# The last graph-attention layer: five weight-side fills instead of nine, the residual product in each unit, and a new order of the side work

## The reference, cut to what matters

```python
h = jnp.maximum(_layernorm(x), 0.0)
Wh = h @ W                                   # 64 x 64
src = Wh @ a[:64]; dst = Wh @ a[64:]
e = leaky_relu(src[:, :, None] + dst[:, None, :], 0.2)
e = where(adj > 0, e, NEG_INF)
attention = softmax(e, axis=-1)              # 1024 x 1024 per graph
h_prime = einsum('bij,bjf->bif', attention, Wh) + h @ W_res
h_prime = elu(h_prime)
x = x + (h_prime - mean) * rsqrt(var + eps) * gamma + beta
```

## Time and profile before

| what | us |
|---|---|
| median of 3 runs (3599.07 to 3604.4) | 3600.49 |
| the profiled execution's own time | 3603.63 |
| its span | 3601.8 |
| start of the last layer on DVE | 3229.28 |
| first transpose of unit 0 of graph 0 | 3260.52 |
| end of the last unit's product | 3584.23 |

### The profile page before, as it was taken

One profiled execution on the slowest core, in us unless ns is written; L12 is line 12 of the kernel. 1 busy time (PEld: TensorE's weight loads), 2 busy tenths in 40 slices (PEclk: granted clock), 3 DMA queues, 4 the chain that ended last, 5 costly groups with the idle time before them and its releaser, 6 DMA issues. The chain is left out here.

```text
span 3601.8 us, 78158 instructions
## 1 busy us (share of the span) xinstructions
PE 3093.4 (86%) x31127; PEld 1693.5 (47%) x31127; DVE 3058.1 (85%) x4734; ACT 2921.4 (81%) x3521; POOL 1005.8 (28%) x565
## 2 busy tenths in 40 slices
PE   7987998999999969888898898988988988878785
PEld 5664666666666633333333333333333333336664
DVE  6666777777787779999999999999999999965765
ACT  4665777777777759999999999999999999966665
POOL 4433665556655600000000100000000000005654
PEclk9998999999999979999999999999999999988988
DMA  7630000000000000000000000000000000002111
GB/s 244 214 129 20 21 21 21 19 21 20 18 19 23 16 10 10 10 10 10 10 10 10 10 10 10 10 10 10 10 10 10 10 10 10 10 17 59 53 53 36
DMA packets 68315, 111.44 MB, mean 31 GB/s; under 512 B 26372, under 2 KB 26502, under 8 KB 67974
## 3 DMA queue, kind: packets, MB, share of 16 engines
q1 hardware_dynamic: 67974, 106.67, 9.7%
HBM read 86.59 MB, written 18.87 MB: 29 GB/s over the span
## 5 line engine op out<-in xcount | busy, mean ns | idle before, releaser
L1029 ACT ACTIVATE l_scalar_ring<-l_w,l_r 128x1024 f32<-128x1024 f32 x1632 | 1716.8, 1161 | 40.4 <-DVE l_values L1075 29.5
L1143 DVE TENSOR_SCALAR l_vector_ring<-l_w_code,l_r_code 128x2048 f32<-128x2048 f32 x1232 | 1590.0, 1359 | 3.5 <-issue 0.6
L966 PE MATMUL scores<-l_scalar_ring,l_signs 128*32 128x512 f32 x6528 | 791.1, 603 | 93.8 <-ACT l_scalar_ring L1029 93.5
L976 PE MATMUL scores<-l_vector_ring,l_signs_code 128*32 128x512 f16 x9856 | 675.4, 396 | 133.8 <-DVE l_vector_ring L1143 132.9
L242 ACT COPY probs_t<-turned 128x512 f32<-128x512 f32 x576 | 325.6, 589 | 435.0 <-PE turned L201 434.8
L450 POOL TENSOR_TENSOR l_masked<-l_relu,mask 128x1024 f32<-128x1024 f32 x256 | 546.1, 2134 | 421.8 <-ACT l_relu L607 390.4
L976 PEld LDWEIGHTS scores<-l_vector_ring,l_signs_code 128*32 128x32 bf16 x9856 | 243.3, 96 | 586.9 <-DVE l_vector_ring L1143 296.3
L212 PE MATMUL outT<-probs_t,l_values 128*64 128x128 f32 x6144 | 430.5, 283 | 88.0 <-ACT probs_t L242 47.4
L212 PEld LDWEIGHTS outT<-probs_t,l_values 128*64 128x64 f32 x6144 | 341.5, 139 | 239.4 <-DVE l_acc L695 95.4
L269 ACT ACTIVATE l_probs<-l_logits,negmax 128x1024 f32<-128x1024 f32 x384 | 443.8, 1156 | 7.6 <-DVE negmax L260 7.6
L201 PE MATMUL turned<-ident,l_probs 128*128 128x128 f32 x3072 | 428.5, 284 | 12.4 <-issue 7.7
(11 more groups left out here) (249 smaller groups left out, 2909.1 us busy)
## 6 DMA issues: line engine op xcount, KB each, us to landing
mask<-masks_kept SPq DMA_DIRECT2D x192, 256.0 KB, 2.7
l_adj<-adj SPq DMA_DIRECT2D x64, 512.0 KB, 5.8
masks_kept<-l_mask_ring SPq DMA_DIRECT2D x64, 256.0 KB, 4.6
x_res<-x SPq DMA_DIRECT2D x8, 256.0 KB, 5.1
out<-x_res SPq DMA_DIRECT2D x8, 256.0 KB, 2.8
l_h<-l_h SPq DMA_DIRECT2D x8, 128.0 KB, 2.9
l_kl<-l_dh SPq DMA_DIRECT2D x32, 2.0 KB, 1.8
l_kl<-l_dl SPq DMA_DIRECT2D x32, 2.0 KB, 1.8
```

The source lines that it names most:

```text
L966: last = nc.tensor.matmul(s.scores[g * ROWS:(g + 1) * ROWS, buf, half, :], signs[:, window], scalar_ring[:, at % SCALAR_RING, g, halves[ha ...
L976: last = nc.tensor.matmul(s.scores[g * ROWS:(g + 1) * ROWS, buf, half, :], signs_code[:, par, g % 2, window], parts(vector_ring[:, at % VE ...
L1029: last = nc.scalar.activation(scalar_ring[:, at % SCALAR_RING, g, :], w[:, par, :], ACT.Relu, bias=r[:, par, column:column + 1])
L1143: last = nc.vector.tensor_scalar(vector_ring[:, at % VECTOR_RING, g:g + 2, :], w_code[:, par, :, :], r_code[:, par, 0, column:column + 1], ...
```

## The change

W is applied after attention instead of before: the values are ReLU(y) itself, and the second turning matmul, which until now only added two halves, multiplies with W stacked twice (`unit_end`). dst and src come from hT times two small products of W and a, made once at the start (`w_dst`, `w_src`). So five fills stay: turn y (0, 1), dst (2, 3), src (4), one in each of units 0 to 4. ACT's second copy of dst goes (its ReLU now scales `dst_slope` by 4), `take_values` is new on DVE (after unit 5), and hT gets two buffers. The residual h @ W_res of a unit is one more matmul behind its product, in the same PSUM bank; DVE copies both at once (192 columns instead of 128). The reciprocal goes ahead of the unit's copy. POOL works four units ahead instead of five, each mask sum in two halves of 512 columns. The output norm takes until the graph after next: `out_centre` at 2, `out_square` at 5, `out_scale` at 0 of the next graph, `out_gamma` after unit 3 and `out_add` after unit 4 there; the layer norm moves one unit earlier (centre 3, square 4, `layer_norm_scale` after 5, y at 6). `store(b - 3)` is issued in the middle of the mask loads of graph b. Core of the diff:

```diff
-    K = 9
-    RING, AHEAD = 4, 5
+    K = 5
+    RING, AHEAD = 4, 4
...
+        turned_both = sb("turned_both", [P, P + D], F32)
+        residual = s.outT[:, P:P + D]
+        unit_out = s.outT[:, P + D:P + 2 * D]
...
-        def fills_before(n):
-            return min(K, (3 * n + 1) // 2)
+        def fills_at(n, project):
+            return [n] if project and n < K else []
...
+            for to, at in ((w[0:D, :], w_dram), (w[D:P, :], w_dram), (wres[0:D, :], w_res),
...
-            for b in range(2, B):
-                loads(b, 0)
-                store(b - 2)
+            for b in range(1, B):
+                loads(b, 0, NB // 2)
+                if b > 2:
+                    store(b - 3)
+                loads(b, NB // 2)
+            store(B - 3)
...
-                nc.gpsimd.tensor_tensor(base[:, n % RING, :], dst_slope[:, par, :], s.mask[:, n % RING, :], ALU.add
-                                        ).then_inc(sems["base_ready"], 1)
+                for half in range(2):
+                    cols = slice(half * BANK, (half + 1) * BANK)
+                    last = nc.gpsimd.tensor_tensor(base[:, n % RING, cols], dst_slope[:, par, cols], s.mask[:, n % RING, cols], ALU.add)
+                last.then_inc(sems["base_ready"], 1)
...
+                wait(g, sems["out_scaled"], b)
...
-                    if n == 3 and not first:
+                    if n == 0 and before > 1:
+                        out_scale(b - 2)
+                    if n == 2 and before > 0:
                         out_centre(b - 1)
+                    if n == 3 and norm:
+                        layer_norm_centre(g, s, sems, next_norm(s, b), b + 2)
                     if n == 4 and norm:
-                        layer_norm_centre(g, s, sems, next_norm(s, b), b + 2)
-                    if n == 5 and norm:
                         layer_norm_square(g, s, sems, b + 2)
-                    if n == 6 and not first:
-                        out_scale(b - 1)
-                    if n == 7 and norm:
+                    if n == 5 and before > 0:
+                        out_square(b - 1)
+                    if n == 6 and norm:
+                        g.wait_ge(sems["values_ready"], b + 1)
                         layer_norm_apply(g, s, sems, next_norm(s, b), par, b + 2, b * K + 2)
...
+                    last = nc.tensor.matmul(bank[:], w_dst[0:D, :], hT[0:D, par, cols], start=True, stop=True)
...
+                        last = nc.tensor.matmul(bank[:, j:j + 1], hT[0:D, par, j * P:(j + 1) * P], w_src[0:D, :], start=True, stop=True,
+                                                skip_group_check=True)
...
+            def product(par, n, u):
+                pe.wait_ge(sems["half0_copied"], STARTS + u + 1)
+                pe.wait_ge(sems["half1_copied"], STARTS + u + 1)
+                wait(pe, sems["out_copied"], STARTS + u)
+                for j in range(NB):
+                    half = j % 2
+                    nc.tensor.matmul(s.outT[half * D:(half + 1) * D, 0:P], values[:, par, j, :], s.probs_t[:, j, :],
+                                     start=(j < 2), stop=(j >= NB - 2), skip_group_check=True)
+                nc.tensor.matmul(residual, hT[0:D, par, n * P:(n + 1) * P], wres[0:D, :], start=True, stop=True,
+                                 skip_group_check=True).then_inc(sems["out_ready"], 1)
+            def unit_end(u):
+                pe.wait_ge(sems["out_copied"], STARTS + u + 1)
+                wait(pe, sems["unit_done"], STARTS + u)
+                nc.tensor.matmul(unit_out, turned_both[:, 0:P], w[:], start=True, stop=True, skip_group_check=True
+                                 ).then_inc(sems["out_turned"], 1)
...
-                    fills = list(range(fills_before(n), fills_before(n + 1))) if project else []
                     turn_probs(pe, s, sems, probs[:, n % 2, :], u)
                     if not (first and n == 0):
-                        turn_out(pe, s, sems, u - 1, 0, unit_out)
-                    for k in fills[:1]:
+                        unit_end(u - 1)
+                    for k in fills_at(n, project):
                         fill(b + 1, 1 - par, k)
                     wait(pe, sems["unit_done"], STARTS + u)
-                    probs_times_values(pe, s, sems, values[:, par, :, :], u)
-                    for k in fills[1:]:
-                        fill(b + 1, 1 - par, k)
+                    if n == 0:
+                        pe.wait_ge(sems["values_ready"], b + 1)
+                    product(par, n, u)
...
+            nc.tensor.transpose(s.fill[0:D, 0:D], w[0:D, :], s.ident[0:D, 0:D]).then_inc(sems["weights_turned"], 1)
+            pe.wait_ge(sems["weights_ready"], 3)
+            nc.tensor.matmul(s.outT[0:D, 0:P], wT[0:D, :], a_rows[0:D, :], start=True, stop=True, skip_group_check=True)
+            nc.tensor.matmul(s.outT[0:D, P:P + 1], wT[0:D, :], acol[0:D, 0:1], start=True, stop=True, skip_group_check=True
+                             ).then_inc(sems["weights_turned"], 1)
+            for k in range(2):
+                fill(0, 0, k)
+            pe.wait_ge(sems["weights_ready"], 4)
+            for k in range(2, K):
...
-            def take_relu(b, par, n, copied=7):
-                a.wait_ge(sems["fill_copied"], b * K + copied)
+            def take_relu(b, par, n):
+                a.wait_ge(sems["fill_copied"], b * K + K)
                 wait(a, sems["logits_ready"], STARTS + b * NB + n - 1)
-                nc.scalar.activation(relu[n % 2], dst[:, par, :], ACT.Relu, bias=src[:, par, n:n + 1]
...
+                nc.scalar.activation(relu[n % 2], dst_slope[:, par, :], ACT.Relu, bias=src[:, par, n:n + 1],
+                                     scale=1.0 / SLOPE - 1.0).then_inc(sems["relu_ready"], 1)
...
-                        for k in range(fills_before(n), fills_before(n + 1)):
-                            dst_fill(b + 1, 1 - par, k)
...
+                v.wait_ge(sems["fill_ready"], b * K + k + 1)
+                if k < 2:
+                    last = nc.vector.tensor_scalar(hT[0:D, par, cols], bank[0:D, :], 0.0, None, ALU.max)
+                elif k < 4:
...
+            def take_values(b, par):
+                v.wait_ge(sems["y_ready"], b + 1)
+                nc.vector.tensor_scalar(values[:, par, :, :], s.y[:, par, :, :], 0.0, None, ALU.max
+                                        ).then_inc(sems["values_ready"], 1)
...
+            def inverse_sum(n):
+                slot = n % 4
+                nc.vector.reciprocal(s.rinv[:, slot:slot + 1], s.rowsum[:, slot:slot + 1])
             def finish(par, n, u):
                 slot = n % 4
-                nc.vector.reciprocal(s.rinv[:, slot:slot + 1], s.rowsum[:, slot:slot + 1])
-                v.drain()
                 v.wait_ge(sems["out_turned"], u + 1)
...
-                                               in1=residual[:, par, n, :], op0=ALU.mult, op1=ALU.add
+                                               in1=turned_both[:, P:P + D], op0=ALU.mult, op1=ALU.add
...
+            def out_gamma(b):
+                v.wait_ge(sems["out_scaled"], b + 1)
+                nc.vector.tensor_tensor(spread[:, 0, :, :], work[:, 3, :, :], gamma[:].unsqueeze(1).to_broadcast([P, NB, D]), ALU.mult)
...
+                v.drain()
+                nc.vector.tensor_tensor(spread[:, 1, :, :], spread[:, 0, :, :], beta[:].unsqueeze(1).to_broadcast([P, NB, D]), ALU.add)
+                v.drain()
+                nc.vector.tensor_tensor(s.graph(b), s.graph(b), spread[:, 1, :, :], ALU.add).then_inc(sems["x_done"], 1)
...
+                    v.drain()
                     if n > 0:
                         finish(par, n - 1, u - 1)
-                    elif not first:
+                    elif before > 0:
                         finish(1 - par, NB - 1, u - 1)
                     if n + 2 < NB or project:
                         logit((n + 2) % NB, u + 2)
-                    for k in fills[:1]:
+                    inverse_sum(n)
+                    v.wait_ge(sems["out_ready"], u + 1)
+                    nc.vector.tensor_copy(turned_both[:], s.outT[:, 0:P + D]).then_inc(sems["out_copied"], 1)
+                    for k in fills_at(n, project):
                         take_fill(b + 1, 1 - par, k)
-                    copy_out(v, s, sems, u)
-                    for k in fills[1:]:
-                        take_fill(b + 1, 1 - par, k)
-                    if n == 0 and not first:
+                    if n == 0 and before > 0:
                         elu(b - 1, 1 - par)
-                    if n == 1 and not first:
+                    if n == 1 and before > 0:
                         out_mean(b - 1)
                     if n == 2 and norm:
                         layer_norm_mean(v, s, sems, next_norm(s, b), b + 2)
-                    if n == 4 and not first:
+                    if n == 3 and before > 1:
+                        out_gamma(b - 2)
+                    if n == 4 and before > 1:
+                        out_add(b - 2)
```

(26 more changed lines are left out.)

111 lines of the change are left out of this document (37 added, 74 removed).

## The result

The changed kernel takes 3588.8 us (median of 6 runs), the kernel before 3602.4 (6 runs): a ratio of 0.9956, 95% interval 0.9938 to 0.9974. That is 14 us faster, where 58 were forecast, and above the range's upper end of 3569. One of the six runs, 5092 us at a much lower clock, is disturbed; the ratio is taken without it, and the median of the other five is 3588.2.

What follows compares the result with a forecast made beforehand. Two chains closing a ring, PE's fills 0 to 5 and POOL's steps to y, were taken to bound the kernel. Graphs -57.7, start -6.1 and clock +6 gave -57.8 us: 3542 us, range 3519 to 3569.

Steps and rivals of the forecast that it cites:

- the ring: Old kernel: fills 0 to 5, then POOL's chain to y, then fill 0; PE waited 3.68 us for y.
- Clock: Low PE clock cost 12 us in two graphs before; part may stay, charged 0 to 12 us, taken as 6.
- Start: Before the first ReLU: fills and W stage go, dst matmuls at low clock +1.7, new steps 1.8; sum -6.1 us.
- Unit 0 and y: Unit 0: y comes 13 to 14 us after dst, wanted at 16.8; wait of 3.68 goes, unit becomes 3.73 us.
- rival 1: Y is still late in unit 0, 3.9 us after PE wants it, 27 us in seven graphs: 3569 us; chance 0.13.
- Residual: Every unit: the residual matmul between product and next transposes adds 0.25 us, unhidden; loop 3.73 instead of 3.48.
- quiet units above 3.8: Sign of being wrong: the residual costs more than 0.25 us per unit, or DVE's wider copy shows.
- Fills: PE's gap between transposes and product: fills 0 to 3 fit within 0.1 us; fill 4 makes unit 4's product 0.9 late.
- Side work: DVE's and ACT's side work: unit 1 +1.3, unit 2 +1.0, unit 5 +0.6 us; 4.2 per graph, full graph 34.0.
- Halving the sums costs nothing: POOL's mask sums: a 512-column operation takes half of 2.14 us, so two halves cost no more than one whole.
- the waits that stand beside the drops go: Clock argument: low clock followed or neighboured PE's waits of 2 to 4 us, which the change removes.
- Rival 3: Low clock makes it slower: 176 us if throughout eight graphs, gain gone at 36% of PE's work; chance 0.04.

Runs made afterwards that it cites:

- e10: Changed kernel with the residual product moved ahead of each unit's eight products, behind its fill: 3549.9 us, 0.9862 of the kernel before.
- e1: Changed kernel with ACT's output exponential in unit 1 moved behind its own exponentials, not ahead of the copies: 3556.9 us, 0.9860 of the kernel before.
- e4: Changed kernel with spare matmuls nobody reads in PE's waits, 8 ahead of fill 1 and 16 in unit 5: 3567.8 us, 0.9899 of the kernel before.
- e6: e4 with POOL's mask sums whole again, 1024 columns instead of two halves: 3583.8 us, 0.9946 of the kernel before.
- e9: e3 with the residual product also moved ahead of the unit's products: 3535.7 us, 0.9823 of the kernel before.
- e3: Changed kernel with the exponential later in unit 1 and out_add's addition to x moved to unit 7: 3551.7 us, 0.9850 of the kernel before.
- e5: e3 with 8 spare matmuls in each of units 5, 6 and 7: 3552.3 us, 0.9859 of the kernel before.
- e8: Kernel before the change with 20 spare matmuls in unit 0 ahead of fill 0, where PE waited for y: 3614.6 us, ratio 1.0035.
- e12: Changed kernel with the residual product ahead of the products in all units but 1 and 5: 3565.4 us, 0.9886 of the kernel before.

## Why the prediction was wrong

The direction was right and the mechanism of the ring too; what failed is the step "Clock", which charged 0 to 12 us and took 6, where the low clock cost some 40 (an estimate, under *Clock* below), and behind it the sizes of two units of side work and of the residual.

- *Start*: -6.1 forecast, -8.2 measured. From the product with `a` to ACT's first ReLU it was 18.3 us before and is 10.5 (3234.24 to 3244.70 in the rows below), 7.9 less. The 1.7 us charged for dst at the low clock did not come: L1422 took 1.95 us for its four matmuls, at a PEclk of 1.00. The low level lay on the transposes ahead of it instead (L190, 3.68 us for 16 passes). The new steps ahead of the first fill took 1.68 (3234.24 to 3235.92), against 1.8.

```profile
3234.24 0.28 DVE L1622 TENSOR_SCALAR l_a_rows<-l_ones,l_acol 64x128 f32<-64x128 f32 x1 [8.44 <-DMA l_beta<-L_gnn_beta]
...
3235.92 3.68 PE L190 MATMUL scores<-ident,y 128*64 128x128 f32 x16
...
3240.47 1.95 PE L1422 MATMUL scores<-l_hT,l_w_dst 64*128 64x512 f32 x4 [0.87 <-DVE l_hT L1524]
...
3244.70 2.15 ACT L1487 ACTIVATE scores<-l_dst_slope,l_src 128x1024 f32<-128x1024 f32 x2 [22.15 <-DVE l_src L1528]
```

- *Unit 0 and y*: right. The wait of 3.68 us went, unit 0 is 3.69 (3.73 forecast); rival 1 is out.
- *Residual*: on the path, as said, but 0.36 us and not 0.25, and 3.84 for a clean unit. It was scaled from 16 passes of equal shape. The prediction's own sign, "quiet units above 3.8", came. It also took the place for given: e10 shows that 1.2 us of idle PE stood beside it in the same unit.
- *Fills*: right. Unit 4 is 4.45 us against 4.63, unit 3 is 3.91 against 3.93.
- *Side work*: unit 2 right (4.66 against 4.73). Unit 1 was 6.22 against 5.03, and unit 5 5.58 (in e1) against 4.33. In both the duration of the unblocked operation was taken (0.79 from L818 to the exponential, 0.76 for each operation of `out_add`), and both operations of the pair were held up, by a mask sum each (0.64 and 1.37 us, 1.38 and 1.39). The 0.79 came from a kernel in which POOL never ran beside L819. The prediction had the blocking in hand, and its bound "+0.1 to 1.1" for unit 5 counted one delay, not two. These two units make 2.4 us, and the full graph is 36.0 us instead of 34.0 (e4, with e1's unit 5). The Trainium skill (SBUF — State Buffer, SBUF: two separate sides) says that DVE, in an operation with two SBUF inputs or in a 2-port mode, and GpSimd share a pair of ports, and that whichever starts first has the pair for its whole instruction. The trace agrees for `out_add`, 1.38 and 1.39 us against 0.69 free, and also L819 with its one input took 1.37 against 0.41; in which mode it ran no row shows.
- *Halving the sums costs nothing*: right as it stands. But it is worth 16 us (e6 against e4), of which the sum had only a part, in unit 2.
- *Clock*: the eight graphs took 324.2 us against a forecast of 266.0 (272.0 with the 6 charged). Keeping PE busy in its waits takes 31 us off between the two traces and 21 between the medians (e4). With the spare matmuls' own 9 us taken out, the low clock costs some 40 of the 58, and some 18 are sizes; both are estimates. The argument was that "the waits that stand beside the drops go". They did go, but the change made new ones of 1.9 to 2.9 us in units 1 and 5, from its own side work. Rival 3 named the outcome, with its chance of 0.04. PEclk 0.80 means the low level for 40% of the stretch, which is 25% of PE's work there, and at the rival's own price (176 us for all of it) 44 us. The rival's text set 36% of the work beside 18% before, and these are different shares: the 18% are of time, and some 10% of the work. So the result lies between the forecast and rival 3, and that it came out below the time of before owes 8 us to the start.

The two mistakes are linked: the list of delays per unit was read as microseconds only, each some 1 to 2, and not also as waits of PE, which here set how often the low level came. Once both waits and the residual are mended (e9), the eight graphs take 266.6 us, with PEclk still at 0.92. That this is the forecast's 266.0 is chance: e9's clean units are 3.39 us and not 3.73.

Not settled is what decides between two equal waits: in graphs 2 and 4 of the changed kernel waits of 2.34 and 2.53 us in unit 1 brought no long stretch, in graphs 1, 3 and 5 waits of 1.94 and 2.56 us did. Nor do the runs part long waits from idle time in sum: shortening the two long waits brought PEclk only to 0.89 (e3), and spare matmuls in the 1.2 us waits of units 5 to 7 brought it on to 0.96 (e5).

## What to carry to other kernels

When a change removes one long wait of PE, list PE's waits that it leaves or makes, unit by unit, and price the clock by them: here 21 us came back by filling two waits of 2 to 3 us per graph, although the filling of unit 5 was 0.6 us too long. Put short matmuls whose operands are early into the place where PE waits for another engine, rather than behind the product that the next loop waits for: the same 0.4 us of work per unit cost 39 us there, more than half of it by the clock. Spare matmuls should be shorter than the wait, counted in passes: in e5 they cost what they gave, in e8 they only stood in the way. And when side work on DVE runs beside POOL's sums, count every operation of it as blocked once, not the group.

## What the runs showed of the hardware

- The granted clock stayed at the 1.2 GHz level for 26, 35 and 43 us in one piece (PEclk 0.51 to 0.54) while PE was recorded busy for 25.0 of 26.1, 32.5 of 34.8 and 39.3 of 42.5 us. High recorded activity did not by itself bring the full level back; in e12 PE was recorded busy for all of 19.91 us at a PEclk of 0.62.
- More work can be faster: 24 spare matmuls per graph took 21 us off the kernel (e4). In e5 and e8, where they were longer than the waits in most of their units, they took nothing off.
- A matmul of 128x128 in f32 counts as two passes: 16 took 3.79 us, 20 took 4.68, at the full clock.
- DVE operations on 128x512 in SBUF took 1.37 to 1.39 us beside mask sums on POOL and 0.41 to 0.69 without.
- A small residual product of two passes of 64 columns took 0.36 us of PE behind the unit's products, and moving it shortened the unit by 0.44.
